# Transposing the router's gates one unit later, into the bank of output 0, in an FFN, attention, FFN kernel

## The reference

```
x = x + 0.5 * ffn(layernorm(x))
x = x + attention(layernorm(x))        # 16 heads, key size 16, value size 64
x = x + 0.5 * ffn(layernorm(x))

ffn:  probs = softmax(flat @ Wr + br)             # 8 experts
      vals, idx = top_k(probs, 2); w = vals / (sum(vals) + EPS)
      out = sum over e of  w_e * (gelu(flat @ W1[e] + b1[e]) @ W2[e] + b2[e])     # W1: 128 x 512, W2: 512 x 128
```

## Time and profile before

| | value |
|---|---|
| median of 3 executions | 797.97 us (797.12 to 799.83) |
| profiled execution, its own time | 799.08 us |
| its span, first to last instruction | 797.3 us |
| PE busy | 776.5 us (97%) |
| DVE busy | 676.5 us (85%) |
| ACT busy | 615.9 us (77%) |
| POOL busy | 201.3 us (25%) |
| mean granted TensorE clock | 0.989 of full speed |

### The profile page before, as it was taken

The page is one execution under the profiler, slowest core; times in us unless marked ns, Lnnn a source line. Parts: engine busy times, 40 slices in busy tenths (PEclk is TensorE's granted clock), DMA queues, the critical chain, the costliest instruction groups (busy, mean ns, idle before and its releaser), DMA issues.

```text
span 797.3 us, 11852 instructions
## 1 busy us (share of the span) xinstructions
PE 776.5 (97%) x3638; PEld 467.6 (59%) x3638; DVE 676.5 (85%) x1347; ACT 615.9 (77%) x1018; POOL 201.3 (25%) x262
## 2 busy tenths in 40 slices
PE   7989999999979999999999999999999899999998
PEld 5868888888763333333333332333498688888886
DVE  7878887889747999999999999999647878878786
ACT  4868676676646999999999999999715676767763
POOL 3116523343300111111111112111112037333331
PEclk8999999999998999999999999999999999999999
DMA  6041312110483111111311111110000133202111
GB/s 176 1 162 53 107 54 106 53 53 1 155 287 87 53 54 53 54 54 53 106 54 54 53 54 53 53 54 1 2 1 1 35 128 115 96 8 99 54 53 53
DMA packets 26437, 54.66 MB, mean 69 GB/s; under 512 B 6288, under 2 KB 11792, under 8 KB 24336
## 3 DMA queue, kind: packets, MB, share of 16 engines
q1 hardware_dynamic: 26384, 54.00, 20.4%
HBM read 44.42 MB, written 9.57 MB: 68 GB/s over the span
## 4 chain that ended last, share of the span: by engine, by line
PE 89%; DVE 5%; DMA 2%; ACT 1%; SPq 1%; issue 1%; POOL 0%; DVEq 0%; ACTq 0%
PE ps L930 29%; PE ps L918 10%; PE ps L368 7%; PE ps L369 7%; PE ps L379 7%; PE ps L370 7%; PE ps L380 7%; PE ps L381 7%; PE ps L937 4%; DMA w2raw<-in_w 1%; PE ps L350 1%; DVE hlo L645 1%; ACT ef L1021 1%; DMA xt<-in_x 1%; PE ps L903 1%
## 5 line engine op out<-in xcount | busy, mean ns | idle before, releaser
L1087 DVE TENSOR_SCALAR_CACHE_REDUCE ef<-ps 128x1024 f32<-128x1024 f32 x256 | 307.4, 1214 | 7.9 <-PE ps L918 1.4
L1021 ACT ACTIVATE ef<-ef,nmax 128x1024 f32<-128x1024 f32 x256 | 293.9, 1148 | 8.9 <-DVE ef L1087 2.3
L930 PE MATMUL ps<-ef,vs 128*64 128x512 f32 x1024 | 249.5, 608 | 0.2
L454 ACT ACTIVATE ps<-ps,b_sb 128x512 f32<-128x512 f32 x256 | 169.0, 663 | 94.4 <-PE ps L370 92.5
L645 DVE TENSOR_TENSOR hlo<-ps,hhi 128x512 fp32r<-128x512 f32 x256 | 165.6, 686 | 5.0 <-ACT ps L454 0.7
L930 PEld LDWEIGHTS ps<-ef,vs 128*64 128x64 f32 x1024 | 62.9, 136 | 121.0 <-issue 108.4
L641 DVE CAST hhi<-ps 128x512 fp32r<-128x512 f32 x128 | 87.7, 685 | 53.2 <-ACT ps L454 53.2
L1126 POOL TENSOR_TENSOR vs<-V,rsum 128x128 f32<-128x128 f32 x128 | 51.1, 400 | 303.0 <-DVE rsum L1093 303.0
L501 POOL TENSOR_TENSOR acc<-acc,ysc 128x512 f32<-128x512 f32 x55 | 70.7, 1288 | 150.8 <-DVE ysc L668 150.1
L368 PE MATMUL ps<-xhi,w1lo 128*128 128x512 f32 x256 | 102.8, 402 | 0.7 <-DVE hlo L645 0.7
L379 PE MATMUL ps<-hhi,w2lo 128*128 128x512 f32 x256 | 101.4, 396 | 0.8 <-DVE gT L716 0.8
(11 more groups left out here) (98 smaller groups left out, 674.4 us busy)
## 6 DMA issues: line engine op xcount, KB each, us to landing
gb<-gates SPq DMA_DIRECT2D x16, 1024.0 KB, 4.7
qs<-qk_parts SPq DMA_DIRECT2D x64, 128.0 KB, 2.5
ks<-qk_parts SPq DMA_DIRECT2D x64, 128.0 KB, 2.6
w1raw<-in_w SPq DMA_DIRECT2D x16, 256.0 KB, 4.9
w2raw<-in_w SPq DMA_DIRECT2D x16, 256.0 KB, 5.4
qk_parts<-sthi SPq DMA_DIRECT2D x16, 256.0 KB, 2.5
qk_parts<-stlo SPq DMA_DIRECT2D x16, 256.0 KB, 3.0
xt<-in_x SPq DMA_DIRECT2D x4, 256.0 KB, 4.0
```

The source lines that it names most:

```text
L454: nc.scalar.activation(bank(mc), bank(mc), ACT.Gelu, bias=b1_sb[:, u, mc:mc + 1]).then_inc(F.gelu, 1)
L930: last = nc.tensor.matmul(bank(6 + half)[x * VD:(x + 1) * VD, :], vs[:, t % VRING, x * VD:(x + 1) * VD], ef[:, (2 * t + x) % ERING, half * ...
L1021: nc.scalar.activation(ef[:, c, :], ef[:, c, :], ACT.Exp, scale=-1.0, bias=nmax[:, c:c + 1], accum_out=esum[:, c:c + 1]).then_inc(s_exp, 1)
L1087: nc.vector.tensor_scalar(ef[:, c, :], bank(slot_bank(u), 2), -1.0, None, ALU.mult, ALU.min, accum_out=nmax[:, c:c + 1]).then_inc(s_max, 1)
```

## The change

On PE, `output(0, 3)` and `hidden(0, 5)` are moved ahead of the wait for the gates; `output(0, 3)` now waits for `F.sh` (the logits in bank 5 have been read). The transpose goes to columns 0 to 127 of bank 4, the bank of outputs 0 and 4, and therefore waits for the end of `back(0, 0)`. `output(0, 4)` follows the copy. On DVE, `front(0, 4)` is moved ahead of the router's last five operations and takes them in, one behind each of its own operations; then come `back(0, 1)` and the copy of the gates. SP, ACT and POOL keep their programs.

```diff
@@ PE, first() @@
                 hidden(0, 4)
+                pe.wait_ge(F.sh, 1)
+                output(0, 3)
+                hidden(0, 5)
                 pe.wait_ge(F.g, 1)
-                nc.tensor.transpose(bank(5)[:, P:2 * P], gte[:, :, :].rearrange("p e t -> p (e t)"),
+                pe.wait_ge(F.scaled, S0 + 1)
+                nc.tensor.transpose(bank(Y_BANKS[0])[:, 0:P], gte[:, :, :].rearrange("p e t -> p (e t)"),
                                     ident).then_inc(F.gT, 1)
                 pe.wait_ge(F.gTs, 1)
-                output(0, 3)
-                for s in range(4, 2 * GR):
+                output(0, 4)
+                for s in range(5, 2 * GR):
                     hidden(0, s + 1)
                     output(0, s)
@@ DVE, first() @@
                 front(0, 3, gates, 2)
                 back(0, 0)
+                front(0, 4, gates, 1)
                 for _ in gates:
                     pass
                 back(0, 1)
                 dve.wait_ge(F.gT, 1)
-                nc.vector.tensor_copy(gT[:, :], bank(5)[:, P:2 * P]).then_inc(F.gTs, 1)
-                front(0, 4)
-                for s in range(2, 2 * GR):
+                nc.vector.tensor_copy(gT[:, :], bank(Y_BANKS[0])[:, 0:P]).then_inc(F.gTs, 1)
+                front(0, 5)
+                back(0, 2)
+                for s in range(3, 2 * GR):
                     front(0, s + SKEW)
                     back(0, s)
```

## The result

The changed kernel takes 807.27 us (median of 4 executions, 806.13 to 808.34) against 798.17 us for the kernel before beside it: 1.0118 times as long, 95% interval 1.0095 to 1.0141. That is 9.1 us slower, where 8.0 us (806.0) was forecast. Measured once more, on another chip (the last experiment), the same two kernels were 12.0 us apart (808.07 and 796.11), so the cost is known only as 9 to 12 us. The profiled execution took 806.3 us with a span of 804.5 us.

A forecast was written before the change was run, and what follows sets the result against it. PE, 97% busy, was taken as the bound, with the gates' copy delaying expert 2's weights through SP's queue. Shifts of 4.0 and 2.6 us plus 1.4 for the clock made 8.0 us, 806.0 us; 8-in-10 range 803.0 to 810.0.

The forecast's parts named there:

- The bound and the chain: PE busy 97%; the gates' copy leads through SP's queue and w2raw to ACT, then to PE in hidden(0, 7).
- PE at the gates: Around the gates' copy: PE gains 1.5 us, waits for unit 4's last low part, and the copy comes 4.0 us later.
- The first FFN's +4.0: At hidden(0, 7), first FFN: PE waits for unit 6, so the copy's whole shift counts, +4.0 us.
- with the same sizes and in the same order: SP's queue behind the gates' copy: everything starts 4.0 us later, otherwise unchanged; expert 2's weights land at 58.3, not 54.28.
- The second FFN's +2.6: At unit 6, second FFN: the 4.0 us shift, less PE's 1.4 us of slack, costs +2.6 us.
- the slack of 1.4 us: Second FFN, chunk 1 of unit 6: low part ready at 648.1, PE takes it at 649.56, leaving 1.4 us.
- The forecast for the median: Whole kernel: 806.0 us from the median 797.97, the profiled execution of 799.08 being 1.1 us above it.
- The clock: Behind PE's new holes at unit 6: half clock on resuming costs 0.7 us per FFN, +1.4 us in all.
- The sum: Whole kernel: 4.0 + 2.6 + 1.4 = 8.0 us slower, giving 806.0 us for the median.
- the clock that stays low longer: Rival, behind the new holes: low clock lasts as near the start, +9.5 to +12 us, about 808.5; chance 15%.
- That the weights do not bind: Rival, unit 6's weights: landing by 52.9, they leave PE's gain standing, -4.8 us, 793.2; chance 4%.
- The pages: DMA queue: descriptors go in ring order, so weights cannot overtake the 2 MB of broadcasts ahead; the shift is whole.

The follow-up runs named there:

- the last experiment: Changed kernel rerun unchanged on another chip, beside one with 23 unread matmuls in PE's wait for unit 6: 808.07 and 806.75 us; kernel before 796.11 us.
- the late store: Kernel before, with one SP wait added so the store of gT and all queued behind it start after unit 4's last low part: 807.34 us, ratio 1.0109.
- the kernel with 23 fillers: Changed kernel with 23 matmuls that nothing reads ahead of hidden(0, 7), where PE waits for unit 6: 806.75 us, beside 808.07 for the changed kernel.
- the kernel with 20 fillers: Changed kernel with 20 matmuls that nothing reads ahead of hidden(0, 7), where PE waits for unit 6: 805.30 us.
- the bank alone: Kernel before with only the transpose put in bank 4, waiting for the end of back(0, 0), nothing moved: 797.06 us, ratio 0.998.
- the first experiment: Changed kernel with the weight loads of experts 2 and 3 moved in SP's queue ahead of its wait for the copied gates: 791.47 us, ratio 0.9915.
- half the delay: Kernel before with the transpose in bank 4 and only output(0, 3) moved ahead of it on PE, DVE's order unchanged: 797.64 us, ratio 1.0005.

## Why the prediction was right, and where it was off

**The bound and the chain.** Right. That the gates' copy leads through SP's queue to ACT and from there to PE was read from the chain of before, and the late store alone brought the whole loss. ACT's waits for w2raw were longer than the 9 and 7 us forecast, 10.1 and 9.1: besides the later landing, ACT is through with unit 5 sooner. Its wait in the first FFN begins 8.2 us behind the anchor instead of 10.8.

**PE at the gates.** Forecast: the copy 4.0 us later, between 3.8 and 4.3. Measured from the anchor it went from 2.93 us (40.60 to 43.53) to 6.66 (39.74 to 46.40), 3.7 us later, the same in the second FFN (633.09 to 639.75). The prediction had PE wait for the last low part of unit 4; it did not. Of the five router operations, each priced at 0.20 us, three added only 0.08 to 0.15 us to DVE's passes, so PE ran at its own pace:

```profile
44.50 0.68 DVE L649 TENSOR_TENSOR hlo<-ps,hhi 128x512 fp32r<-128x512 f32 x1
...
45.38 0.39 PE L368 MATMUL ps<-xhi,w1lo 128*128 128x512 f32 x1
```

The low part ends at 45.18, and the last chunk starts at 45.38 with no wait before it. The copy then began 0.31 us behind the transpose (46.09, 46.40), where 0.44 had been counted.

**The first FFN's +4.0.** By the kernel with 23 fillers, in which no clock fall is mixed in, the shift cost 25.09 - 20.55 = 4.5 us. The sum was short by the landing. It was priced with the 7.57 us of before, and took 8.41; with the 3.7 of the copy that is the 4.5. The step "with the same sizes and in the same order" was right on the order and silently took the duration as fixed.

**The second FFN's +2.6.** Right against the profiled execution of the kernel before: 24.01 - 21.29 = 2.7 us, where the first is the kernel with 20 fillers, whose clock stayed up. But the slack of 1.4 us was made by the clock fall in the gates' hole of that execution, which had held PE back by some 1.3 us (from output(0, 3) to hidden(0, 6) it took 4.15 us, and 2.86 with the bank alone). Against the bank alone, whose clock did not fall there, the same shift costs 24.01 - 20.22 = 3.8 us. There PE takes chunk 1 of hidden(0, 7) 0.83 us behind chunk 0, not 0.70, so next to nothing is left of the slack:

```profile
647.46 0.39 PE L368 MATMUL ps<-xhi,w1lo 128*128 128x512 f32 x1
...
648.29 0.50 PE L368 MATMUL ps<-xhi,w1lo 128*128 128x512 f32 x1
```

The forecast for the median took the 1.1 us by which the profiled execution was slow off the time and kept the slack that its fall had made. On the other chip, where most executions of the kernel before had a higher mean clock and were 2 us faster, the two kernels are 12.0 us apart. That these executions were spared the fall at the gates would fit, but is not shown: none of them has a trace here.

**The clock.** This is the mis-sized term. That both new holes would bring the lower level was right. The cost was taken as 0.7 us for each FFN, from the one short low stretch behind the gates' hole, 2.7 us long behind the restart. It lasted 3.4 and 5 us behind the restart and cost 1.0 to 1.55 and 1.8 us, 2.8 or more together against 1.4, inside the bound of 2.7 each.

**The sum.** 4.5 + 2.7 + 2.8 = 10.0 us by the profiles, and 9.1 and 12.0 by the two pairs of medians, for 4.0 + 2.6 + 1.4 = 8.0. In the first FFN two errors offset each other in part, a copy 0.3 us less late and a landing 0.8 us longer. The mechanism was right and the sum was short.

**The rivals.** The one that came nearest is the clock that stays low longer, given 15% and +9.5 to +12 us: both new holes had it, at 3.4 and 5 us behind PE's restart. That the weights do not bind was refuted with numbers that stood up: 6.3 us at the least from copy to landing, 5.3 to be had. With the weights ahead of the broadcasts the queue came to just that. From copy to landing took 5.28 us there (46.87 to 52.15), since the weights' issue came 0.9 us sooner with no broadcast ahead of it, and PE's stall was all but gone. The gain of the rival, 4.8 us for a kernel whose weights do not bind, is what the first experiment shows, and more: 6.8 us. By the ruler 5.4 of it is in the two places (20.55 - 18.23 and 21.29 - 18.22); of the rest, the profile of the kernel before holds the 1.65 us of the clock fall early in attention, which the first experiment's profile has not; by the medians the rest stays open.

**The pages.** The Trainium skill (DMA: Bandwidth & Descriptors, Queues, rings and completion order) has an engine take descriptors in ring order. The measured pair agrees: 8.41 us behind two broadcasts, 3.03 us ahead of them, the same load.

## What to carry to other kernels

A step that fills a hole on the busiest engine may also be the first item in another queue. Before it is delayed, list everything behind it in that queue, down to the loads that have nothing to do with it but stand there, and ask of each who is idle for it already: here ACT's 2.98 us for w2raw said that every microsecond would count in full. Where an engine seems to have slack, see whether a clock fall in that one execution made it: the 1.4 us of the second FFN were of that kind. And put loads that depend on nothing ahead of the wait of those that do: this one move turned +9.1 us into -6.8 us, though in the kernel before, where PE had nothing to gain from it, it was worth too little to tell (ratio 0.9985).

## What the runs showed of the hardware

The landing of the same load, w2raw of expert 2, behind the same two broadcasts, was not fixed: 7.57 us in the first FFN of the kernel before, 7.50 with half the delay and with the bank alone, 8.40, 8.41, 8.36 and 9.08 in the kernels whose store was late, and 7.27 to 8.52 in the second FFN of the late ones. The kernel of before with the store late shows 8.40 too, so the order on PE and DVE isn't the reason. Nor is it more traffic: between 38 and 62 us the kernel before, the changed one, the one with the store late and the one with 20 fillers all moved the same 1154 packets, 3.24 MB. What it is stays open.

A hole of PE of 2.5 us sometimes takes the clock down and sometimes doesn't: in the kernel before in the second FFN and not in the first, and in the kernel before with the weights early in the first and not in the second, with the bank alone in neither. The holes of 5 and 6 us of the changed kernel took it down in all four profiled cases. In the kernel with the late store, whose holes are 4.5 and 3.7 us, it was still at full speed when PE resumed, and fell 0.8 and 1.6 us later: in the first FFN the first chunk behind the hole still runs at full speed (0.23 us from its second matmul to its third), and the second at 0.43 us a matmul.

```profile
62.34 0.50 PE L369 MATMUL ps<-xhi,w1lo 128*128 128x512 f32 x1 [4.48 <-DVE hlo L646]
62.68 0.40 PE L370 MATMUL ps<-xlo,w1hi 128*128 128x512 f32 x1
...
63.66 0.79 PE L369 MATMUL ps<-xhi,w1lo 128*128 128x512 f32 x1 [0.36 <-DVE hlo L646]
64.26 0.63 PE L370 MATMUL ps<-xlo,w1hi 128*128 128x512 f32 x1
```
